# A two-layer LSTM step: forget gate first, input and candidate gate packed in one bank, and x multiplied inside the recurrence

## The reference, cut to what matters

```python
def _lstm_cell(x, h, c, Wi, Wh, bi, bh):
    g = x @ Wi.T + bi + h @ Wh.T + bh
    i, f, gg, o = jnp.split(g, 4, axis=-1)
    c2 = jax.nn.sigmoid(f) * c + jax.nn.sigmoid(i) * jnp.tanh(gg)
    h2 = jax.nn.sigmoid(o) * jnp.tanh(c2)
    return (h2, c2)

def step(carry, x_t):
    h0, c0, h1, c1, a = carry
    xin = jnp.concatenate([x_t, a], axis=-1)
    h0, c0 = _lstm_cell(xin, h0, c0, Wi0, Wh0, bi0, bh0)
    h1, c1 = _lstm_cell(h0, h1, c1, Wi1, Wh1, bi1, bh1)
    q = h1 @ Wq.T
    attn = jax.nn.softmax(jnp.einsum('bh,bsh->bs', q, context), axis=-1)
    mixed = jnp.einsum('bs,bsh->bh', attn, context)
    a2 = jnp.tanh(jnp.concatenate([mixed, h1], axis=-1) @ Wo.T + bo)
    return ((h0, c0, h1, c1, a2), a2)
```

## Time and profile before

| | us |
|---|---|
| median of 3 runs (8883.11 to 8890.32) | 8883.31 |
| the profiled execution | 8888.59 |
| its span, first to last instruction | 8886.8 |
| preparation (until 37.5) | 37.5 |
| input gates (37.5 to 165.8) | 128.3 |
| recurrence (first DMA of gx to its last a) | 7515.8 |
| everything behind the recurrence | 1202.1 |

### The profile page before, as it was taken

The page is one execution under the profiler, slowest core; times in us unless marked ns, Lnnn a source line. Parts: engine busy times, 40 slices in busy tenths (PEclk is TensorE's granted clock), DMA queues, the critical chain, the costliest instruction groups (busy, mean ns, idle before and its releaser), DMA issues. The chain is left out here.

```text
span 8886.8 us, 624664 instructions
## 1 busy us (share of the span) xinstructions
PE 7041.0 (79%) x278357; PEld 5474.4 (62%) x278365; DVE 4208.4 (47%) x21242; ACT 2138.4 (24%) x11947; POOL 280.8 (3%) x295
## 2 busy tenths in 40 slices
PE   7888888888888888888888888888888888576777
PEld 4666666666666666666666666666666666453455
DVE  5444444444444444444444444444444444566812
ACT  1222222222222222222222222222222222222322
POOL 0000000000000000000000000000000000112411
PEclk9999999999999999999999999999999999788788
DMA  3000000000000000000000000000000000000233
GB/s 130 2 2 2 2 2 2 2 2 2 2 2 2 2 2 2 2 2 2 2 2 2 2 2 2 2 2 2 2 2 2 2 2 2 25 6 17 75 135 112
DMA packets 99290, 127.30 MB, mean 14 GB/s; under 512 B 30880, under 2 KB 83512, under 8 KB 98360
## 3 DMA queue, kind: packets, MB, share of 16 engines
q1 hardware_dynamic: 96184, 118.49, 4.1%
q0 software_dynamic: 3072, 8.39, 0.3%
HBM read 91.14 MB, written 35.65 MB: 14 GB/s over the span
## 5 line engine op out<-in xcount | busy, mean ns | idle before, releaser
L393 PE MATMUL scan_sums_if<-rec_wh,scan_hT 128*4 128x128 f32 x32752 | 1457.5, 273 | 0.0
L520 DVE STREAM_TRANSPOSE scan_sums_if<-scan_sums_if 128x128 f32<-128x128 f32 x2048 | 679.1, 332 | 1200.1 <-PE scan_sums_if L393 1200.1
L393 PE MATMUL scan_sums_o<-rec_wh,scan_hT 128*4 128x64 f32 x32752 | 1133.8, 219 | 0.0
L393 PE MATMUL scan_sums_if<-rec_wi,scan_hT 128*4 128x128 f32 x16384 | 635.0, 273 | 502.5 <-DVE scan_hT L527 502.5
L464 ACT ACTIVATE scan_tanh_if<-scan_sums_if 128x16 f32<-128x16 f32 x2048 | 377.3, 184 | 2543.5 <-DVE scan_sums_if L520 2543.5
L393 PE MATMUL scan_sums_g<-rec_wh,scan_hT 128*4 128x64 f32 x32752 | 946.5, 219 | 0.0
L393 PE MATMUL scan_sums_if<-rec_wa,scan_aT 128*4 128x128 f32 x16384 | 635.5, 273 | 273.4 <-ACT scan_aT L477 273.4
L402 PE MATMUL scan_scores<-rec_kp,scan_hT 128*4 128x64 f32 x16384 | 416.3, 219 | 510.0 <-DVE scan_hT L527 510.0
L393 PEld LDWEIGHTS scan_sums_if<-rec_wi,scan_hT 128*4 128x4 f32 x16384 | 331.9, 85 | 696.2 <-DVE scan_hT L527 691.5
L393 PEld LDWEIGHTS scan_sums_g<-rec_wh,scan_hT 128*4 128x4 f32 x32752 | 719.1, 87 | 9.0
L393 PEld LDWEIGHTS scan_sums_if<-rec_wh,scan_hT 128*4 128x4 f32 x32752 | 719.0, 87 | 4.5
(11 more groups left out here) (292 smaller groups left out, 12301.2 us busy)
## 6 DMA issues: line engine op xcount, KB each, us to landing
scan_gx<-gx_scratch SPq DMA_DIRECT2D x4096, 4.0 KB
experts_bias<-in_b SPq DMA_DIRECT2D x40, 640.0 KB, 3.8
gx_scratch<-gx_out SPq DMA_DIRECT2D x32, 512.0 KB, 2.9
moe_w<-in_w SPq DMA_DIRECT2D x16, 1024.0 KB, 12.5
...
```

What stands on the lines that cost most here:

```text
L393: last = nc.tensor.matmul(sums[layer][g][32 * j:32 * j + B, 0:WIDTH[g]], state[:, k, 0:B], weight[:, k, j, COLUMNS[g]], start=start and k ...
L520: nc.vector.transpose(turned[l][g], sums[l][g][:, 0:WIDTH[g]]).then_inc(gates_turned[l][g], 1)
```

## The change

- The order of the gates in all weights becomes f, i, g, o. Bank f holds f alone (64 columns). Bank ig holds i and g packed by rows: the state tiles become 12 columns wide with the state in the middle and zeros around it, and an 8-column stationary operand (`FIRST`, `ROWS`) puts i on rows 0 to 3 and g on rows 4 to 7 of each block of 32, in the same 64 columns. A product is 4 gates of 8 matmuls, all of 64 columns.
- VectorE turns f, then ig (64 columns each), multiplies 1 + tanh(f) by c (8 elements), turns o. One tanh on ScalarE takes i and g together (16 elements) and writes them into the scan's input, whose 4 elements per value form the product i*g and the sum; the scan is 32 elements, with add before multiply. Three semaphores (of tanh f, of the scan's terms, of the two factors of h) take the place of five.
- `input_gates` becomes `turn_inputs`: it only normalizes and turns x, and keeps it turned in on-chip memory (`xT_all`). In the recurrence ScalarE copies the step's 8 elements per partition (`take_x`), behind the tanh that makes a, and TensorE multiplies them by `wx`: 32 matmuls a step (gate f ahead of the wait for the softmax, i, g and o behind `vp`), where `add_gx` had 12. The DMAs of a step are gone.
- The biases of layer 0 come in as four seeds of its own a step (`seed_gates(0)`, behind `wi1`), layer 1 has four seeds instead of three.
- `wh1` and `wh0` are no longer split into chunks over several places.

```diff
-                in_steps(pe, [(turn, 0), (product, 1)])
+                in_steps(pe, [(turn, 0)])
...
+                    nc.scalar.activation(xT_all[:, :, bass.ds(g * B * P + P * b, P)],
+                                         turned[b % 2][:, 0:D].rearrange("p (c n) -> p c n", c=KC), ACT.Copy).then_inc(xT_done, 1)
...
-                in_steps(dve, [(moments, 0), (normalize, 1), (evacuate, 3)])
+                in_steps(dve, [(moments, 0), (normalize, 1)])
...
+        F, IG, O = range(3)
+        GATE_F, GATE_I, GATE_G, GATE_O = range(GATES)
+        BANK = (F, IG, IG, O)
+        ROWS = (B, 2 * B, 2 * B, B)
+        FIRST = (B, B, 0, B)
+        sums = [[m.psum(f"sums{l}_{g}") for g in ("f", "ig", "o")] for l in range(2)]
...
+        flat = [t[:].rearrange("p f k b e -> p f (k b e)") for t in scanned]
+        forget_term = [t[:, 0].rearrange("p k b e -> p (k b) e")[:, :, 3] for t in scanned]
+        ig_terms = [t[:].rearrange("p f k b e -> p k f b e")[:, :, :, :, 2] for t in scanned]
+        tanh_f = [m.sbuf(f"tanh_f{l}", [P, 2, B]) for l in range(2)]
         tanh_o = [m.sbuf(f"tanh_o{l}", [P, 2, B]) for l in range(2)]
-        hT = [m.sbuf(f"hT{l}", [P, 2, B]) for l in range(2)]
-        aT = m.sbuf("aT", [P, 2, B])
+        hT = [m.sbuf(f"hT{l}", [P, 2, 3 * B]) for l in range(2)]
+        aT = m.sbuf("aT", [P, 2, 3 * B])
+        xT = [m.sbuf(f"xT{i}", [P, 2, 3 * B]) for i in range(2)]
...
+                def product(layer, state, weight, gates=(GATE_F, GATE_I, GATE_G, GATE_O), done=None):
+                    for g in gates:
+                        for k in range(2):
                             for j in range(4):
-                                last = nc.tensor.matmul(sums[layer][g][32 * j:32 * j + B, 0:WIDTH[g]], state[:, k, 0:B],
-                                                        weight[:, k, j, COLUMNS[g]], start=start and k == 0,
-                                                        stop=stop and k == 1, skip_group_check=True)
-                        if done is not None:
-                            last.then_inc(done[g], 1)
+                                last = nc.tensor.matmul(sums[layer][BANK[g]][32 * j:32 * j + ROWS[g], 0:64],
+                                                        state[:, k, FIRST[g]:FIRST[g] + ROWS[g]],
+                                                        weight[:, k, j, 64 * g:64 * g + 64], start=False,
+                                                        stop=done is not None and g != GATE_I and k == 1, skip_group_check=True)
+                        if done is not None and g != GATE_I:
+                            last.then_inc(done[BANK[g]], 1)
...
+                def seed_bias(bank, at, rows=w["sel"], start=True):
+                    nc.tensor.matmul(bank[:, 0:64], rows[:], bias_parts[:, 64 * at:64 * at + 64], start=start, stop=False,
+                                     skip_group_check=True)
+                def seed_gates(layer):
+                    at = BIAS_AT[layer]
+                    seed_bias(sums[layer][F], at + GATE_F)
+                    seed_bias(sums[layer][IG], at + GATE_I)
+                    seed_bias(sums[layer][O], at + GATE_O)
+                    seed_bias(sums[layer][IG], at + GATE_G, w["sel_high"], False)
+                def step(t, s, last=False):
                     n = t + s + 1
                     pe.wait_ge(a_ready, n)
-                    product(0, aT, w["wa"], stop=True, done=gates_summed[0])
-                    product(1, hT[1], w["wh1"], chunks=(1,))
-                    product(1, hT[1], w["wh1"], groups=(G, O), chunks=(0,))
+                    product(0, aT, w["wa"], done=gates_summed[0])
+                    product(1, hT[1], w["wh1"])
                     pe.wait_ge(h_ready[0], n + 1)
-                    product(1, hT[0], w["wi1"], stop=True, done=gates_summed[1])
+                    product(1, hT[0], w["wi1"], done=gates_summed[1])
                     if not last:
-                        product(0, hT[0], w["wh0"], groups=(IF, G), start=True)
+                        seed_gates(0)
+                        product(0, hT[0], w["wh0"], (GATE_F, GATE_I, GATE_G))
                     pe.wait_ge(h_ready[1], n + 1)
-                    head_product(scores, hT[1], w["kp"], True, True).then_inc(scores_done, 1)
-                    seed_bias(a_sum, slice(256, 320))
-                    head_product(a_sum, hT[1], w["woh"], False, False)
+                    head_product(scores, state_of(hT[1]), w["kp"], True, True).then_inc(scores_done, 1)
+                    seed_bias(a_sum, GATES)
+                    head_product(a_sum, state_of(hT[1]), w["woh"], False, False)
                     if not last:
-                        product(0, hT[0], w["wh0"], groups=(O,), chunks=(0,), start=True)
...
-                            seed_bias(sums[1][g], COLUMNS[g])
-                        pe.wait_ge(gx_loaded[(s + 1) % U], loaded)
-                        add_gx((s + 1) % U, False)
+                        product(0, hT[0], w["wh0"], (GATE_O,))
+                        seed_gates(1)
+                        pe.wait_ge(x_ready, n + 1)
+                        product(0, xT[(s + 1) % 2], w["wx"], (GATE_F,))
                     pe.wait_ge(probs_ready, n)
-                    head_product(a_sum, pT, w["vp"], False, True).then_inc(a_summed, 1)
+                    head_product(a_sum, pT[:], w["vp"], False, True).then_inc(a_summed, 1)
                     if not last:
-                        product(0, hT[0], w["wh0"], groups=(O,), chunks=(1,))
-                        product(1, hT[1], w["wh1"], groups=(IF,), chunks=(0,))
+                        product(0, xT[(s + 1) % 2], w["wx"], (GATE_I, GATE_G, GATE_O))
...
+                def take_x(t, s):
+                    nc.scalar.activation(state_of(xT[s]), xT_all[:, :, bass.ds((t + s) * B, B)], ACT.Copy).then_inc(x_ready, 1)
                 def step(n):
                     for l in range(2):
...
+                        act.wait_ge(gates_turned[l][F], n)
+                        nc.scalar.activation(tanh_f[l][:], gates_of[l][F][:, :, 0:B], ACT.Tanh).then_inc(f_tanh[l], 1)
+                        act.wait_ge(gates_turned[l][IG], n)
+                        nc.scalar.activation(ig_terms[l], gates_of[l][IG][:, :, 0:2 * B].rearrange("p k (f b) -> p k f b", f=2),
+                                             ACT.Tanh).then_inc(c_terms[l], 1)
                         act.wait_ge(gates_turned[l][O], n)
-                        nc.scalar.activation(tanh_o[l][:], gatesT[l][O][:, 0], ACT.Tanh).then_inc(o_tanh[l], 1)
+                        nc.scalar.activation(tanh_o[l][:], gates_of[l][O][:, :, 0:B], ACT.Tanh).then_inc(h_factors[l], 1)
...
+                def turn(l, g, n):
+                    dve.wait_ge(gates_summed[l][g], n)
+                    nc.vector.transpose(turned[l][g], sums[l][g][:, 0:64]).then_inc(gates_turned[l][g], 1)
                 def step(t, s):
                     n = t + s + 1
                     for l in range(2):
...
+                        turn(l, F, n)
+                        turn(l, IG, n)
+                        dve.wait_ge(f_tanh[l], n)
+                        nc.vector.scalar_tensor_tensor(forget_term[l], tanh_f[l][:].rearrange("p k b -> p (k b)"), 1.0, c_of[l],
+                                                       ALU.add, ALU.mult).then_inc(c_terms[l], 1)
+                        turn(l, O, n)
+                        dve.wait_ge(c_terms[l], 2 * n)
+                        nc.vector.tensor_tensor_scan(cell[l], flat[l][:, 0], flat[l][:, 1], 0.0, ALU.add, ALU.mult).then_inc(c_done[l], 1)
+                        dve.wait_ge(h_factors[l], 2 * n)
+                        nc.vector.scalar_tensor_tensor(state_of(hT[l]), tanh_o[l][:], 1.0, tanh_c[l].rearrange("p (k b) -> p k b", k=2),
+                                                       ALU.add, ALU.mult).then_inc(h_ready[l], 1)
```

More of the change, by code:

```diff
@@ L141, in _ @@
                     rows = slice(32 * p, 32 * p + 4)
-                    sp.dma_start(bias[0][rows, 0:GATES, :], ins["bi1"]).then_inc(bias_in, 16)
-                    sp.dma_start(bias[1][rows, 0:GATES, :], ins["bh1"]).then_inc(bias_in, 16)
+                    for l in range(2):
+                        gates = slice(BIAS_AT[l], BIAS_AT[l] + GATES)
+                        sp.dma_start(bias[0][rows, gates, :], ins[f"bi{l}"]).then_inc(bias_in, 16)
+                        sp.dma_start(bias[1][rows, gates, :], ins[f"bh{l}"]).then_inc(bias_in, 16)
                     sp.dma_start(bias[0][rows, GATES, :], ins["bo"]).then_inc(bias_in, 16)
@@ L261, in turn @@
                     last.then_inc(turned_done, 1)
-                def product(g, b):
-                    pe.wait_ge(xT_done, number(g, b) + 2)
-                    pe.wait_ge(out_done, number(g, b))
-                    for h in range(2):
-                        for c in range(KC):
```

(41 more changed lines are left out.)

205 lines of the change are left out of this document (71 added, 134 removed).

## The result

| | before | after |
|---|---|---|
| median of 4 runs each | 8883.21 us (8881.65 to 8890.32) | 8625.74 us (8623.44 to 8627.25) |
| profiled execution: span | 8886.8 us | 8621.7 us |
| ratio, 95% interval | | 0.9708 (0.9692 to 0.9725) |

The account below looks back on a forecast made before the run. The recurrence, one chain of latencies of 7.334 us a step, was taken as the bound, not TensorE. 8888.6 - 164 (gate order) - 87 (front) - 2 = 8635.6, 8630 as median; range 8560 to 8770, own range 8565 to 8705.

Parts of the forecast that it names:

- the order of the gates: Recurrence, both layers: f first and the packed bank gain 0.08 us a layer, 0.16 a step, 164 us.
- The chain of a layer: Recurrence: turns at 0.47, 0.91, 1.16, scan at 1.43 instead of 1.52, next product at 2.14 us.
- The scan has 32 elements for 24 ... I take 0.01: VectorE's scan in each layer: 8 more elements cost 0.01 us, bounded at 0.04.
- If fewer semaphores to wait for save 0.02: Each layer: fewer semaphores might save 0.02 us, only in the upper end of 0.11 a layer.
- h1 to a: From the start of h1's product to that of a's, in each step: still 2.89 us.
- Idle 0.12, the narrowest cover: TensorE's queue behind vp: 0.88 us of work against 1.00 until the next product with a.
- Packed gates, 8 wide: TensorE loads 8 columns wide: taken as costing nothing, upper end 0.03 us for a packed bank.
- the 8848 of that rival: Packed gates' loads not hidden behind streaming: 0.053 us a packed gate, 0.21 a step, 8848 us; x = 0.05 had chance 0.03.
- Ahead of the recurrence: Input stage without its product: 41 us instead of 128.3, gain 87; earlier first matmul of the recurrence, gain 2.
- Front only: Rival: the front gains, the recurrence does not; 8794 us, range 8705 to 8860, chance 0.15.

Follow-up runs that it names:

- the new cell with the old waits: Kernel before with the changed cell (f first, i and g packed), front and gx as before, h and softmax waiting for two semaphores each: 8851.79 us, ratio 0.9957.
- the experiment in the kernel before: Kernel before with its scan over 32 elements instead of 24, the last 8 idle: 8920.55 us, ratio 1.0038.
- the run with the old cell: Changed kernel's turn_inputs and product with wx, but the cell of the kernel before (banks if, g, o, unjoined semaphores, scan of 24): 8802.3 us, ratio 0.9897.

## Why the prediction was right, and where it wasn't

The time was hit to 4 us, but that is luck in good part: the front gave what was said, while of the 164 us that the prediction gave to the order of the gates only 41 came from it. The joined waits gave 207, the longer steps behind the jump took 67 back, and 41 + 207 - 67 = 181 lies close to 164 by chance.

- *The chain of a layer.* Turns at 0.48, 0.92 and 1.15 for 0.47, 0.91 and 1.16, scan at 1.46 for 1.43, next product at 2.13 for 2.14. The scan is what I said comes last. But the 0.08 a layer that I gave to the order is 0.02 by the new cell with the old waits. The scan starts 0.06 earlier than before and its result comes 0.04 later behind its start.
- *"The scan has 32 elements for 24 ... I take 0.01"*: it measured 0.04 more to tanh of c, the end of my bound. The elements are 0.017 of it (the experiment in the kernel before); the rest goes, in the main, with the scan's later start behind the turn (it no longer overlaps it), which I hadn't thought of.
- *"If fewer semaphores to wait for save 0.02"*: the mis-sized term. It stood only at the upper end, for a layer. It is 0.07 for each joined wait, in each layer and at pT: 0.20 to 0.215 a step, 207 to 220 us. That the change also joins the two semaphores ahead of pT stood neither in its description nor in the sum. h1 to a was said to stay at 2.89; it is 2.81 where no jump stands in it.
- *"Idle 0.12, the narrowest cover"* behind vp: the place was right. The jump at the loop's end wasn't in the sum: 0.13 at 511 steps, 67 us, on which the experiment with gate i ahead got 71 back. Ahead of vp I gave 0.39 of idle time; it held gate i (0.22) and about 0.1 more, as the run with all of x ahead shows.
- *Packed gates, 8 wide.* A packed gate streams in 0.22 like any other (the turn of ig comes 0.44 behind that of f, with two gates between). The page after, by form (busy us, mean ns, idle before):

```profile
L334 PE MATMUL scan_sums_ig<-rec_wh,scan_hT 128*8 128x64 f32 x65504 | 1291.2, 219 | 2.8 <-issue 2.8
L334 PEld LDWEIGHTS scan_sums_ig<-rec_wh,scan_hT 128*8 128x8 f32 x65504 | 1026.8, 90 | 3.2 <-issue 3.2
...
L334 PE MATMUL scan_sums_o<-rec_wh,scan_hT 128*4 128x64 f32 x32752 | 833.9, 219 | 3.0 <-issue 3.0
...
L334 PEld LDWEIGHTS scan_sums_o<-rec_wh,scan_hT 128*4 128x4 f32 x32752 | 563.4, 87 | 3.3 <-issue 3.3
```

  The load is 3 to 4 ns longer, about what the rule of the Trainium skill gives (TensorE: Matmul & The Clock Gate, section on LDWEIGHTS). But it stands beside the streaming, so the 8848 of that rival did not come.
- *Ahead of the recurrence*: 42.8 us where 41 were forecast; in all 89.8 us where 87 + 2 were.
- *"Front only"* (8794): the run with the old cell, 8802, is that case. The kernel after with split waits, 8847, is beyond it. Had the joined waits not been part of the change, this rival (8705 to 8860) would have held the time, and the forecast's range would not.
